# Attention scores from f16 halves: three products in place of one f32 product

## The chip, the cores and the metric

The kernel runs on one core of one Trainium2 chip. The core has five engines that each work through a queue of their own in order and meet through semaphores: TensorE (PE; its weight loads are shown apart as PEld), VectorE (DVE), ScalarE (ACT), GpSimd (POOL) and SyncE (SP, which only starts transfers). The metric is the device time of one launch in microseconds, lower is better.

## The reference

`x` is (4, 1024, 256) f32, the context (4, 64, 256). One layer, in two halves:

```
q = layernorm(x) @ w_qs[h]          # 16 heads of 64
k, v = ctx @ w_ks[h], ctx @ w_vs[h]
attn = softmax(q @ k.T)             # over the 64 context rows, no scaling
out = (attn @ v) * q                # times q, elementwise
x = x + tanh(g_xattn) * (concat(out) @ w_proj.T + b_proj)
logits = layernorm(x) @ gate_w.T    # 8 experts, the best 2 per token
y = sum over the 2 of softmax weight * (silu(x @ w1[e]) @ w2[e])
x = x + tanh(g_ffn) * y
```

The result is compared at f32 precision, so a product of two f32 matrices is either run in f32 or as three products of f16 halves (high by high, high by low, low by high).

## The kernel before, in words

**Two stages.** `attention` runs first and takes some 357 us, `experts` follows on the same core and takes the rest (71 blocks of 128 tokens). The change lies in `attention`, but for one call in `experts`.

**Tiling of attention.** The 4096 tokens are 8 groups of 512 (g = 0 to 7), two for each batch row. The 16 heads are 8 pairs (p = 0 to 7); a pair fills 128 partitions. So there are 64 steps, n = 8 g + p, and each engine has a function `step` that is run once for each n. The order inside a step is written out by hand and differs by engine; semaphores (waits like `pe.wait_ge(q_sb, n + 1)`) tie the engines together.

**What belongs to one step n**, by engine and in its order there:

- TensorE: q of pair n in six f16 products (L604); the scores of pair n-1 in f32 (`scores`, L614: four products 128x128x128, which the chip runs as eight); the transposes of the probabilities of n-4 (L625); probabilities times V of n-5 (L640); the output projection of n-6 in f16 halves (L656, L665); then a small job that depends on p (routing of group g-2, turning the next group's x).
- ScalarE: q from PSUM to f32 (`copy_q`, L816); copy of the transposed probabilities (L821); exponentials of n-2 (L826); at p 0, 1, 4 and 5 two LayerNorm tiles; the high half of a piece of an expert's weights (L867); the high half of the product of n-5 (`product_hi`, r_h, L832).
- VectorE: the sum of exponentials and its reciprocal, n-3 (L1021, L1024); LayerNorm and residual work by p; maximum and subtraction on the scores of n-1 (`score_max` L1010, `score_sub` L1015), with small routing jobs in the gaps between (`between`, gaps 1 to 4); attention times q, n-5 (`times_q`, r, L1030); the low half of the weight piece (L1067).
- GpSimd: probabilities normalized, n-3 (L1300); at p 3 and 7 an inverse deviation (L1278); one scatter of token records to memory (L1316), the first of a group behind the row numbers (`slots_done`); then the low half of the product of n-5 (`product_lo`, r_l, L1306), which waits for r_h.

Scores are single-buffered: `scores` waits until `score_sub` has read the pair before. The f32 K of all pairs, `kb`, is built in group 0 by `place_k` (ScalarE the lower, VectorE the upper 64 partitions).

**Routing of a group** runs two groups later: logits at p 2, best two experts at p 3, `both_masks` at p 4, and at p 5 `place_rows` (gap 1), `record_weights` (gap 2), `pick_rows` (gap 3, its first line updates `next_row`, which frees a PSUM bank that TensorE needs for turning x) and `row_numbers` (gap 4).

Of the kernel before, what the change touches and what calls it, by code (L numbers as in the profile page):

```python
# [30 lines left out]
P = 128  # L31
# [213 lines left out]
                            carry.next_row[:, :].unsqueeze(1).broadcast_to([P, TG, E]), ALU.add).then_inc(s.route_ops, 1)  # L245


def pick_rows(nc, dve, job_ps, r, s, carry, g):
    dve.wait_ge(s.route_ops, g * ROUTE + 5)
    nc.vector.tensor_tensor(carry.next_row[:, :], job_ps[:, TG * E:(TG + 1) * E], carry.next_row[:, :], ALU.add).then_inc(s.pos_read, 1)  # L250
    nc.vector.tensor_tensor(r.mask[:, :, :, :], r.pos[:, :, :].unsqueeze(1).broadcast_to([P, 2, TG, E]), r.mask[:, :, :, :],
                            ALU.mult).then_inc(s.route_ops, 1)

# [16 lines left out]
def attention(nc, ctx, dram, carry, weights):  # L270
# [8 lines left out]
    def sb(name, shape, dt):  # L279
        return ctx.enter_context(nc.sbuf_tensor(name, shape, dt))  # L280
# [4 lines left out]
    def sem(name):  # L285
        return ctx.enter_context(nc.semaphore(name))
# [1 line left out]

    wq_h, wq_l = (sb(f"wq_{s}", [P, KD, H * DK], F16) for s in "hl")
    wp_h, wp_l = (sb(f"wp_{s}", [P, NP, D], F16) for s in "hl")  # L290
    kb = sb("kb", [P, B, NP, 2 * M], F32)
    vb = sb("vb", [P, B, NP, 2, DK], F32)
    bias_rows = sb("bias_rows", [P, D], F16)
    bias_high = sb("bias_high", [64, D], F16)
# [15 lines left out]
    xn = carry.xn  # L310
    xt_h, xt_l = (sb(f"xt_{s}", [P, 2, KD, G], F16) for s in "hl")
    q32 = sb("q32", [P, NP, G], F32)
    smax = sb("smax", [P, 2, TG, 2], F32)
    ssub = sb("ssub", [P, 2, TG, 2, M], F32)
    ex = sb("ex", [P, 2, TG, 2 * M], F32)
# [51 lines left out]
        "base_set", "consts_set", "k_zeroed", "setup_ops", "tanh_done", "first_rows"))  # L367
    wp_hi, wp_lo, wq_hi, wq_lo, bias_hi = (sem(n) for n in ("wp_hi", "wp_lo", "wq_hi", "wq_lo", "bias_hi"))
    bias_zeroed, bias_lo = sem("bias_zeroed"), sem("bias_lo")
    k_mm, k_placed, v_mm, v_placed = (sem(n) for n in ("k_mm", "k_placed", "v_mm", "v_placed"))  # L370
    ln1_ops, ln1_rstd, ln1_shift, xn_done, xt_tp, xt_hi, xt_lo = (sem(n) for n in ("ln1_ops", "ln1_rstd", "ln1_shift", "xn_done", "xt_tp", "xt_hi", "xt_lo"))
    last_r_lo = sem("last_r_lo")
    q_mm, q_sb, s_mm, s_max, s_sub, e_x, pt_mm, e_sb = (sem(n) for n in (
# [166 lines left out]
    def _(pe):  # L540
# [22 lines left out]
        def project_k(p):  # L563

            pe.wait_ge(ctx_in, 16)
            pe.wait_ge(wk_in, 16)
            if p >= len(K_AT[0]):
                pe.wait_ge(k_placed, 2 * p)
# [37 lines left out]
            last.then_inc(q_mm, 1)  # L606

        def scores(b, n, p):
            pe.wait_ge(q_sb, n + 1)
            if isinstance(n, int) and n < NP:  # L610
                pe.wait_ge(k_placed, 2 * n + 2)
            after(pe, s_sub, n)
            for t in range(TG):
                last = nc.tensor.matmul(s_ps[:, t].rearrange("p h m -> p (h m)"), q32[:, p, t * P:(t + 1) * P],  # L614
                                        kb[:, b, p, :] if isinstance(b, int)
                                        else kb[:, bass.ds(b, 1), p, :].rearrange("p o m -> p (o m)"),
                                        start=True, stop=True)
# [68 lines left out]
        def small_job(g, k, p):  # L686

            if p == 1 and known(g, 2):
                x2_transpose(g - 2, k, 0)
            if p == 2 and known(g, 2):  # L690
                logits(g - 2)
            if p == 4 and known(g, 2):
                positions(g - 2)
            if p == 5 and has_next(g):
                if known(g, 2):
                    pe.wait_ge(routed.pos_read, g - 1)
                elif g == 0:
                    pe.wait_ge(k_placed, 2 * NP)
# [55 lines left out]
    def _(act):  # L754
# [35 lines left out]
        def place_k(p):  # L790

            act.wait_ge(k_mm, p + 1)
            if p == 0:
                act.wait_ge(k_zeroed, 2)
            nc.scalar.copy(k_place(kb, p, 0), k_batches(p, 0)).then_inc(k_placed, 1)

        def place_v(part):

# [10 lines left out]
        def copy_q(n, p):  # L809
# [5 lines left out]
            after(act, r_mul, n - NP + 1)  # L815
            nc.scalar.mul(q32[:, p, :], q_ps[:, :], 1.0 / WS).then_inc(q_sb, 1)  # L816

        def probs_out(n, p):
            act.wait_ge(pt_mm, n + 1)
            after(act, ot_mm, n - 1)  # L820
            nc.scalar.copy(e32[:, p % 2, :], pt_ps[:, :]).then_inc(e_sb, 1)  # L821

        def exps(n, p):
            act.wait_ge(s_sub, n + 1)
            after(act, p_nrm, n - 1)
            nc.scalar.activation(ex[:, p % 2].rearrange("p t m -> p (t m)"),  # L826
                                 ssub[:, p % 2].rearrange("p t h m -> p (t h m)"), ACT.Exp).then_inc(e_x, 1)
# [41 lines left out]
        def step(b, g, k, p, pairs_back=LAST):  # L869
# [64 lines left out]

    @block.vector
    def _(dve):
        nc.vector.memset(kb[:, 0:B // 2].rearrange("p b n m -> p (b n m)").bitcast(U32), 0).then_inc(k_zeroed, 1)
        nc.vector.memset(bias_rows[:, :].bitcast(U32), 0).then_inc(bias_zeroed, 1)

        def ln1(g, par):  # L940
# [54 lines left out]
        def place_k(p):  # L995

            dve.wait_ge(k_mm, p + 1)
            if p == 0:
                dve.wait_ge(k_zeroed, 2)
            nc.vector.tensor_copy(k_place(kb, p, 1), k_batches(p, 1)).then_inc(k_placed, 1)  # L1000

        def split_wp(part):

# [121 lines left out]
        def between(g, k, p, gap):  # L1125
# [14 lines left out]
            if p == 3:  # L1140
# [5 lines left out]
                    best_experts(nc, dve, route, routed, g - 2)  # L1146
                if gap == 4:
                    choice_masks(nc, dve, route, routed, carry, g - 2)
            if p == 4 and gap == 1:
                both_masks(nc, dve, route, routed, g - 2)  # L1150
            if p == 5:
                if gap == 1:
                    place_rows(nc, dve, job_ps, route, routed, carry, g - 2)
                if gap == 2:
                    record_weights(nc, dve, route, routed, carry, g - 2, rec[k])
                if gap == 3:
                    pick_rows(nc, dve, job_ps, route, routed, carry, g - 2)
# [75 lines left out]
        for p in range(LAST):  # L1233
            n = NS + p
            if p < 3:
                exp_sum(n - 3, NP + p - 3)
            if p < 1:
                score_max(n - 1, NP + p - 1)
                score_sub(n - 1, NP + p - 1)
            if p == 2:  # L1240
                dve.wait_ge(carry.rows_in[0], BLOCK_LOADS)
                turn_rows(nc, carry.xt, carry.rows, 0).then_inc(carry.x_turned, 1)
            if p < 5:
                times_q(n - 5, NP + p - 5)
# [14 lines left out]
    def _(pool):  # L1259
# [59 lines left out]
        def step(g, k, p, pairs_back=LAST):  # L1319
# [37 lines left out]
def experts(nc, ctx, dram, carry, loads_base, weights):  # L1357
# [240 lines left out]
    def _(dve):  # L1598
# [54 lines left out]
        def routing(j, i):  # L1653
# [24 lines left out]
            if i == 7:  # L1678
# [134 lines left out]
```

## Time and profile before

| what | value |
|---|---|
| median of three runs | 757.85 us (756.53 to 765.16) |
| the profiled execution | 760.15 us, its span 758.4 us |
| TensorE busy | 728.1 us (96% of the span) |
| VectorE busy | 586.2 us (77%) |
| ScalarE busy | 377.6 us (50%) |
| GpSimd busy | 397.4 us (52%) |
| mean granted TensorE clock | 0.995 |
| f32 score products L614 | 512, 67.5 us busy |

The busy times are sums over both stages, and a busy TensorE counts its products from start to end although they overlap. For the change only attention's stretch matters, and in it the place of each step: when its scores start, and when the last piece of GpSimd's work of that step ends.

### The profile page before, as it was taken

What the parts mean: (1) busy time and instruction counts of PE and PEld (TensorE: products, weight loads), DVE (VectorE), ACT (ScalarE), POOL (GpSimd) and SP (SyncE); (2) the same over time, 40 slices, a digit from 0 to 9 for tenths busy, and PEclk for the clock granted to TensorE, in tenths of its full rate; (3) what the DMA queues carried; (4) which work ended last, traced back from release to release, by engine and by line L of the source; (5) the groups of instructions that cost most, each with busy time, mean ns of one, the idle gap of its engine ahead of it and who ended that gap; (6) DMA issues with size and microseconds to landing.
All of it is one profiled execution on the core that took longest, in us unless ns stands there. A gap on an engine that the chain in (4) does not pass through costs nothing.

```text
span 758.4 us, 23508 instructions
## 1 busy us (share of the span) xinstructions
PE 728.1 (96%) x7980; PEld 605.2 (80%) x7981; DVE 586.2 (77%) x1270; ACT 377.6 (50%) x671; POOL 397.4 (52%) x308
## 2 busy tenths in 40 slices
PE   7999999999999999998899999999999999999994
PEld 6567767767677766776899988999999999999993
DVE  5688879798897989796778778776767677777761
ACT  3686776767677667754344432333333333333331
POOL 5145445767576666674533648444444353444434
PEclk9999999999999999999999999999999999999998
DMA  8552353536282625433888885333333333333322
GB/s 293 161 145 108 140 167 116 180 128 225 77 286 78 231 98 182 153 116 93 254 224 223 228 205 123 53 52 50 49 49 49 50 47 54 49 51 49 51 37 29
DMA packets 93177, 93.88 MB, mean 124 GB/s; under 512 B 59312, under 2 KB 77936, under 8 KB 92720
## 3 DMA queue, kind: packets, MB, share of 16 engines
q1 hardware_dynamic: 31184, 64.97, 25.8%
q0 software_dynamic: 13392, 18.03, 13.7%
q10 hardware_dynamic: 48528, 9.92, 7.6%
q8 instruction: 43, 0.70, 0.4%
q14 instruction: 30, 0.25, 0.1%
HBM read 53.89 MB, written 37.95 MB: 121 GB/s over the span
## 4 chain that ended last, share of the span: by engine, by line
DMA 40%; issue 7%; POOL 3%; PE 1%; ACTq 1%; DVE 1%; ACT 1%; POOLq 0%; DVEq 0%
DMA out<-y,meta 40%; POOL records L1757 2%; POOL out L1751 1%; PE h_ps L1484 0%; ACTq L158 0%; ACT y L1556 0%; ACT hid L1549 0%; PE h_ps L1528 0%; DVE last_stats L1659 0%; DVE ht_l L1629 0%; POOLq L70 0%; ACTq L160 0%; DVE ht_h L1627 0%; ACTq L1535 0%; DVE bx L165 0%
## 5 line engine op out<-in xcount | busy, mean ns | idle before, releaser
L1751 POOL DMA_INDIRECT out<-y,meta x71 | 157.4, 2217 | 198.4 <-DMA out<-y,meta 178.8
L1484 PE MATMUL h_ps<-bx_h,w_now 128*128 128x128 f16 x2272 | 194.7, 219 | 3.0 <-DVE bx_l L1615 1.6
L1497 PE MATMUL pair_ps<-weights,ht_h 128*128 x1136 | 190.7, 273 | 1.9 <-issue 1.3
L1484 PEld LDWEIGHTS h_ps<-bx_h,w_now 128*128 128x128 f16 x2272 | 152.6, 98 | 6.8 <-DVE bx_l L1615 2.6
L1484 PE MATMUL h_ps<-bx_l,w_now 128*128 128x128 f16 x1136 | 156.4, 219 | 0.9 <-issue 0.9
L1497 PE MATMUL pair_ps<-weights,ht_l 128*128 x568 | 154.8, 273 | 0.0
L1497 PEld LDWEIGHTS pair_ps<-weights,ht_h 128*128 128x128 f16 x1136 | 110.2, 97 | 17.9 <-issue 3.4
L1556 ACT ACTIVATE y<-pair_ps,meta 128x256 f32<-128x256 f32 x71 | 33.7, 475 | 172.3 <-DVE meta L1610 114.8
L1306 POOL TENSOR_TENSOR r_l<-r,r_h 128x512 f16<-128x512 f32 x62 | 75.3, 1215 | 73.6 <-ACT r_h L832 71.7
L1627 DVE CAST ht_h<-hid 128x1024 f16<-128x1024 f32 x71 | 50.1, 706 | 81.5 <-ACT hid L1549 76.6
L1549 ACT ACTIVATE hid<-h_ps 128x1024 f32<-128x1024 f32 x71 | 72.7, 1023 | 62.7 <-PE h_ps L1484 59.6
L1629 DVE TENSOR_TENSOR ht_l<-hid,ht_h 128x1024 f16<-128x1024 f32 x71 | 87.0, 1225 | 2.4
L1484 PEld LDWEIGHTS h_ps<-bx_l,w_now 128*128 128x128 f16 x1136 | 87.3, 98 | 0.8 <-issue 0.8
L1621 DVE COPY w_now<-weights 128x4096 f16 x71 | 87.3, 1229 | 0.2 <-DVE loads_base L1650 0.2
L1300 POOL TENSOR_TENSOR pn<-ex,rinv 128x512 f32<-128x512 f32 x64 | 66.5, 1039 | 30.9 <-DVE rinv L1024 30.9
L614 PEld LDWEIGHTS s_ps<-kb,q 128*128 128x128 f32 x512 | 67.1, 191 | 9.3 <-issue 0.7
L614 PE MATMUL s_ps<-kb,q 128*128 128x128 f32 x512 | 67.5, 275 | 0.3 <-DVE ssub L1015 0.3
L656 PE MATMUL pair_ps<-wp_h,r_h 128*128 128x256 f16 x256 | 61.3, 275 | 0.8 <-ACT r_h L832 0.8
L656 PE MATMUL pair_ps<-wp_l,r_h 128*128 128x256 f16 x256 | 60.7, 273 | 0.0
L1497 PEld LDWEIGHTS pair_ps<-weights,ht_l 128*128 128x128 f16 x568 | 55.6, 98 | 5.2
L1010 DVE TENSOR_REDUCE smax<-s_ps 128x8 f32<-128x512 f32 x64 | 43.2, 675 | 17.7 <-PE s_ps L614 17.0
L821 ACT COPY e<-pt_ps 128x512 f32<-128x512 f32 x64 | 37.4, 585 | 36.0 <-PE pt_ps L625 36.0
(250 smaller groups left out, 1235.9 us busy)
## 6 DMA issues: line engine op xcount, KB each, us to landing
stage<-in_w SPq DMA_DIRECT2D x16, 1024.0 KB
w_split<-split SPq DMA_DIRECT2D x14, 1024.0 KB, 6.5
weights<-w_split SPq DMA_DIRECT2D x14, 1024.0 KB
rows<-records ACTq DMA_DIRECT2D x268, 32.0 KB
xin<-in_x SPq DMA_DIRECT2D x7, 512.0 KB, 5.4
x_even<-in_x SPq DMA_DIRECT2D x4, 512.0 KB
x_odd<-in_x SPq DMA_DIRECT2D x4, 512.0 KB
out<-x_even SPq DMA_DIRECT2D x4, 512.0 KB
```

What stands on the lines that cost most here:

```text
L614: last = nc.tensor.matmul(s_ps[:, t].rearrange("p h m -> p (h m)"), q32[:, p, t * P:(t + 1) * P], kb[:, b, p, :] if isinstance(b, int) els ...
L656: nc.tensor.matmul(pj_ps[:, t, :], r_h[:, p % 2, t * P:(t + 1) * P], wt[:, p, :], start=(p == 0 and i == 0 and t % 2 == 0), stop=False, sk ...
L1010: nc.vector.tensor_reduce(smax[:, p % 2], s_ps[:, :, :, :], AX.X, ALU.max).then_inc(s_max, 1)
L1300: nc.gpsimd.tensor_tensor(pn[:, p % 2].rearrange("p h t m -> p t h m"), ex[:, p % 2].rearrange("p t (h m) -> p t h m", h=2), rinv[:, p % 2 ...
L1306: nc.gpsimd.tensor_tensor(r_l[:, p % 2, :], r32[:, p % 2, :], r_h[:, p % 2, :], ALU.subtract).then_inc(r_lo, 1)
L1484: last = nc.tensor.matmul(h_ps[r % 2][:, c, :], w1_now[:, r % 2, s, k * F + c * P:k * F + c * P + P], xt[:, r % 2, k, :], start=(j == 0 an ...
L1497: last = nc.tensor.matmul(y_ps[r % 2], ht[:, r % 2, c, :], weights_at(e, s, WN // 2 + c * D, D).rearrange("p o n -> p (o n)"), start=(c == ...
L1549: nc.scalar.activation(hid[:, r % 2], h_ps[r % 2][:, :, :], ACT.Silu, scale=1.0 / WS).then_inc(h_act, 1)
L1621: nc.vector.tensor_copy(w1_now[:, r % 2], weights[:, bass.ds(e, 1), :, 0:KD * F].rearrange("p o s n -> p (o s) n")).then_inc(w1_ready, 1)
L1627: nc.vector.tensor_copy(ht_h[:, r % 2], hid[:, r % 2]).then_inc(h_hi, 1)
L1629: nc.vector.tensor_tensor(ht_l[:, r % 2], hid[:, r % 2], ht_h[:, r % 2], ALU.subtract).then_inc(h_lo, 1)
L1751: pool.indirect_dma_start(out, bass.IndirectOffsetOnAxis(meta[:, r, 0:1].bitcast(U32), 0), y[:, r % 2, :], None, compute_op=ALU.add).then_ ...
```

## The change

Scores become three f16 products. `q_high` (ScalarE, behind `copy_q`) makes q_h = f16(q32); `q_low` (GpSimd, the last instruction of its step) makes q_l = f16(q32 - q_h). K is kept as two f16 arrays scaled by 64 (`WS`), and the exponential divides by 64. TensorE first runs eight products with q_h (for K's high and low half), then waits for q_l and runs four more with K's high half. The other part moves three small jobs on VectorE: `place_rows` from p 5, gap 1 to p 4, gap 4; the `next_row` update from `pick_rows` into `count_rows` at p 5, gap 1; and in the drain after the last group the rest of the block table goes to earlier steps, ahead of a wait for rows.

```diff
-def pick_rows(nc, dve, job_ps, r, s, carry, g):
+def count_rows(nc, dve, job_ps, s, carry, g):
+    dve.wait_ge(s.route_ops, g * ROUTE + 5)
+    nc.vector.tensor_tensor(carry.next_row[:, :], job_ps[:, TG * E:(TG + 1) * E], carry.next_row[:, :], ALU.add).then_inc(s.pos_read, 1)
+def pick_rows(nc, dve, r, s, g):
...
-    kb = sb("kb", [P, B, NP, 2 * M], F32)
+    kb_h, kb_l = (sb(f"kb_{s}", [P, B, NP, 2 * M], F16) for s in "hl")
+    q_h, q_l = (sb(f"q_{s}", [P, 2, G], F16) for s in "hl")
...
         def scores(b, n, p):
-            pe.wait_ge(q_sb, n + 1)
+            pe.wait_ge(q_hi, n + 1)
...
             for t in range(TG):
-                last = nc.tensor.matmul(s_ps[:, t]..., q32[:, p, t * P:(t + 1) * P], kb[:, b, p, :], start=True, stop=True)
+                for i, kb in enumerate((kb_h, kb_l)):
+                    nc.tensor.matmul(s_ps[:, t]..., q_h[:, p % 2, t * P:(t + 1) * P], kb[:, b, p, :],
+                                     start=(i == 0 and t == 0), stop=False, skip_group_check=True)
+            pe.wait_ge(q_lo, n + 1)
+            for t in range(TG):
+                last = nc.tensor.matmul(s_ps[:, t]..., q_l[:, p % 2, t * P:(t + 1) * P], kb_h[:, b, p, :],
+                                        start=False, stop=True, skip_group_check=True)
             last.then_inc(s_mm, 1)
...
+        def q_high(n, p):                        # ScalarE, in step n right behind copy_q
+            act.wait_ge(q_sb, n + 1)
+            after(act, s_mm, n - 1)
+            nc.scalar.copy(q_h[:, p % 2, :], q32[:, p, :]).then_inc(q_hi, 1)
...
         def place_k(p):                          # VectorE; ScalarE's: mul by WS into kb_h, then_inc(k_hi)
-            nc.vector.tensor_copy(k_place(kb, p, 1), k_batches(p, 1)).then_inc(k_placed, 1)
+            nc.vector.tensor_scalar(k_place(kb_h, p, 1), k_batches(p, 1), WS, None, ALU.mult).then_inc(k_upper, 1)
+            dve.wait_ge(k_hi, p + 1)
+            nc.vector.scalar_tensor_tensor(k_place(kb_l, p, 0), k_batches(p, 0), WS, k_place(kb_h, p, 0), ALU.mult, ALU.subtract)
+            dve.wait_ge(k_upper, p + 1)
+            nc.vector.scalar_tensor_tensor(k_place(kb_l, p, 1), ...).then_inc(k_lo, 1)
...
+        def q_low(n, p):                         # GpSimd
+            pool.wait_ge(q_hi, n + 1)
+            after(pool, s_mm, n - 1)
+            nc.gpsimd.tensor_tensor(q_l[:, p % 2, :], q32[:, p, :], q_h[:, p % 2, :], ALU.subtract).then_inc(q_lo, 1)
...
             if pairs_back >= 5:
                 product_lo(n - 5, (p - 5) % NP)
+            q_low(n, p)
...
-            if p == 4 and gap == 1:
-                both_masks(nc, dve, route, routed, g - 2)
+            if p == 4:
+                if gap == 1:
+                    both_masks(nc, dve, route, routed, g - 2)
+                if gap == 4:
+                    place_rows(nc, dve, job_ps, route, routed, carry, g - 2)
             if p == 5:
                 if gap == 1:
-                    place_rows(nc, dve, job_ps, route, routed, carry, g - 2)
+                    count_rows(nc, dve, job_ps, routed, carry, g - 2)
```

## Rows read from the trace of the kernel before

**Rows 1.** Busy time by stretch; engine columns, TensorE's granted clock, DMA share, GB/s.

```profile
8.00:10.00 2.00, 1.02 (x9) 0.82 (x7) 0.77 (x4) 0.43 (x1) 1.77 (x8) 1.00 1.02 416
...
259.70:301.20 41.50, 40.52 (x346) 29.11 (x345) 35.97 (x98) 29.37 (x54) 27.95 (x28) 1.00 0.46 154
```

**Rows 2.** Timeline, TensorE's scores, group 6 and the next start; start, length, us.

```profile
259.67 1.05 PE L614 MATMUL s_ps<-kb,q 128*128 128x128 f32 x8
264.31 1.05 PE L614 MATMUL s_ps<-kb,q 128*128 128x128 f32 x8
269.77 1.05 PE L614 MATMUL s_ps<-kb,q 128*128 128x128 f32 x8
275.50 1.05 PE L614 MATMUL s_ps<-kb,q 128*128 128x128 f32 x8
280.13 1.05 PE L614 MATMUL s_ps<-kb,q 128*128 128x128 f32 x8
284.88 1.05 PE L614 MATMUL s_ps<-kb,q 128*128 128x128 f32 x8
...
291.50 1.05 PE L614 MATMUL s_ps<-kb,q 128*128 128x128 f32 x8
...
296.61 1.05 PE L614 MATMUL s_ps<-kb,q 128*128 128x128 f32 x8
301.24 1.05 PE L614 MATMUL s_ps<-kb,q 128*128 128x128 f32 x8
```

**Rows 3.** Timeline, GpSimd's r_l of the same eight steps; last, idle before it.

```profile
264.41 1.15 POOL L1306 TENSOR_TENSOR r_l<-r,r_h 128x512 f16<-128x512 f32 x1 [0.42 <-ACT r_h L832]
...
269.30 1.15 POOL L1306 TENSOR_TENSOR r_l<-r,r_h 128x512 f16<-128x512 f32 x1 [1.58 <-ACT r_h L832]
...
274.01 1.15 POOL L1306 TENSOR_TENSOR r_l<-r,r_h 128x512 f16<-128x512 f32 x1 [1.40 <-ACT r_h L832]
...
279.69 1.58 POOL L1306 TENSOR_TENSOR r_l<-r,r_h 128x512 f16<-128x512 f32 x1 [1.27 <-ACT r_h L832]
...
286.20 1.15 POOL L1306 TENSOR_TENSOR r_l<-r,r_h 128x512 f16<-128x512 f32 x1 [1.81 <-ACT r_h L832]
...
291.95 1.17 POOL L1306 TENSOR_TENSOR r_l<-r,r_h 128x512 f16<-128x512 f32 x1
...
295.74 1.15 POOL L1306 TENSOR_TENSOR r_l<-r,r_h 128x512 f16<-128x512 f32 x1 [0.46 <-ACT r_h L832]
...
302.23 1.17 POOL L1306 TENSOR_TENSOR r_l<-r,r_h 128x512 f16<-128x512 f32 x1
```

**Rows 4.** Timeline, VectorE and ScalarE, the step whose scores start at 291.50.

```profile
293.00 0.68 DVE L1010 TENSOR_REDUCE smax<-s_ps 128x8 f32<-128x512 f32 x1
...
294.32 0.68 DVE L1030 TENSOR_TENSOR r<-ot_ps,q 128x512 f32<-128x512 f32 x1
...
295.03 0.62 ACT L832 CAST r_h<-r 128x512 f16<-128x512 f32 x1 [0.38 <-DVE r L1030]
```

**Rows 5.** Timeline, VectorE's maximum in the steps p 4, 5 and 7.

```profile
282.03 0.64 DVE L1010 TENSOR_REDUCE smax<-s_ps 128x8 f32<-128x512 f32 x1
...
287.08 0.64 DVE L1010 TENSOR_REDUCE smax<-s_ps 128x8 f32<-128x512 f32 x1
...
298.22 0.67 DVE L1010 TENSOR_REDUCE smax<-s_ps 128x8 f32<-128x512 f32 x1
```

**Rows 6.** Timeline, TensorE in the experts' stage, f16 products 128x128x128.

```profile
564.19 0.39 PE L1484 MATMUL h_ps<-bx_h,w_now 128*128 128x128 f16 x4
...
564.53 0.39 PE L1484 MATMUL h_ps<-bx_h,w_now 128*128 128x128 f16 x4
```

**Rows 7.** Groups by line, attention: the same subtraction on VectorE; busy, mean ns.

```profile
L1247 DVE TENSOR_TENSOR r_l<-r,r_h 128x512 f16<-128x512 f32 x2 | 1.4, 692 | 1.4 <-ACT r_h L832 1.4
```

**Rows 8.** Timeline, TensorE's scores: start of group 1 and of group 2.

```profile
54.95 1.05 PE L614 MATMUL s_ps<-kb,q 128*128 128x128 f32 x8
...
93.41 1.05 PE L614 MATMUL s_ps<-kb,q 128*128 128x128 f32 x8
```

More of the change, by code:

```diff
@@ L369, in attention @@
     bias_zeroed, bias_lo = sem("bias_zeroed"), sem("bias_lo")
-    k_mm, k_placed, v_mm, v_placed = (sem(n) for n in ("k_mm", "k_placed", "v_mm", "v_placed"))
+    k_mm, k_hi, k_upper, k_lo, v_mm, v_placed = (sem(n) for n in ("k_mm", "k_hi", "k_upper", "k_lo", "v_mm", "v_placed"))
+    q_hi, q_lo = sem("q_hi"), sem("q_lo")
     ln1_ops, ln1_rstd, ln1_shift, xn_done, xt_tp, xt_hi, xt_lo = (sem(n) for n in ("ln1_ops", "ln1_rstd", "ln1_shift", "xn_done", "xt_tp", "xt_hi", "xt_lo"))
@@ L567, in project_k @@
             if p >= len(K_AT[0]):
-                pe.wait_ge(k_placed, 2 * p)
+                pe.wait_ge(k_lo, p)
             for k in range(KD):
@@ L608, in scores @@
         def scores(b, n, p):
-            pe.wait_ge(q_sb, n + 1)
-            if isinstance(n, int) and n < NP:
-                pe.wait_ge(k_placed, 2 * n + 2)
+            pe.wait_ge(q_hi, n + 1)
+            if n < NP:
+                pe.wait_ge(k_lo, n + 1)
             after(pe, s_sub, n)
             for t in range(TG):
[L614 to L617, printed above, removed]
+                for i, kb in enumerate((kb_h, kb_l)):
+                    nc.tensor.matmul(s_ps[:, t].rearrange("p h m -> p (h m)"), q_h[:, p % 2, t * P:(t + 1) * P], kb[:, b, p, :],
+                                     start=(i == 0 and t == 0), stop=False, skip_group_check=True)
+            pe.wait_ge(q_lo, n + 1)
+            for t in range(TG):
+                last = nc.tensor.matmul(s_ps[:, t].rearrange("p h m -> p (h m)"), q_l[:, p % 2, t * P:(t + 1) * P], kb_h[:, b, p, :],
+                                        start=False, stop=True, skip_group_check=True)
             last.then_inc(s_mm, 1)
@@ L697, in small_job @@
                 elif g == 0:
-                    pe.wait_ge(k_placed, 2 * NP)
+                    pe.wait_ge(k_lo, NP)
                 x_transpose(g + 1, 0, job_ps)
@@ L793, in place_k @@
             if p == 0:
-                act.wait_ge(k_zeroed, 2)
-            nc.scalar.copy(k_place(kb, p, 0), k_batches(p, 0)).then_inc(k_placed, 1)
+                act.wait_ge(k_zeroed, 3)
+            nc.scalar.mul(k_place(kb_h, p, 0), k_batches(p, 0), WS).then_inc(k_hi, 1)
         def place_v(part):
@@ L826, in exps @@
             nc.scalar.activation(ex[:, p % 2].rearrange("p t m -> p (t m)"),
-                                 ssub[:, p % 2].rearrange("p t h m -> p (t h m)"), ACT.Exp).then_inc(e_x, 1)
+                                 ssub[:, p % 2].rearrange("p t h m -> p (t h m)"), ACT.Exp, scale=1.0 / WS).then_inc(e_x, 1)
         def product_hi(n, p):
@@ L879, in step @@
                     place_k(v)
+            q_high(n, p)
             if p == 2 and known(g, 2):
@@ L936, in _ @@
     def _(dve):
-        nc.vector.memset(kb[:, 0:B // 2].rearrange("p b n m -> p (b n m)").bitcast(U32), 0).then_inc(k_zeroed, 1)
+        nc.vector.memset(kb_h[:, :].rearrange("p b n m -> p (b n m)").bitcast(U32), 0).then_inc(k_zeroed, 1)
         nc.vector.memset(bias_rows[:, :].bitcast(U32), 0).then_inc(bias_zeroed, 1)
@@ L998, in place_k @@
             if p == 0:
-                dve.wait_ge(k_zeroed, 2)
-            nc.vector.tensor_copy(k_place(kb, p, 1), k_batches(p, 1)).then_inc(k_placed, 1)
+                dve.wait_ge(k_zeroed, 3)
+            nc.vector.tensor_scalar(k_place(kb_h, p, 1), k_batches(p, 1), WS, None, ALU.mult).then_inc(k_upper, 1)
+            dve.wait_ge(k_hi, p + 1)
+            nc.vector.scalar_tensor_tensor(k_place(kb_l, p, 0), k_batches(p, 0), WS, k_place(kb_h, p, 0), ALU.mult, ALU.subtract)
+            dve.wait_ge(k_upper, p + 1)
+            nc.vector.scalar_tensor_tensor(k_place(kb_l, p, 1), k_batches(p, 1), WS, k_place(kb_h, p, 1), ALU.mult, ALU.subtract).then_inc(k_lo, 1)
         def split_wp(part):
@@ L1156, in between @@
                 if gap == 3:
-                    pick_rows(nc, dve, job_ps, route, routed, carry, g - 2)
+                    pick_rows(nc, dve, route, routed, g - 2)
                 if gap == 4:
@@ L1239, in _ @@
                 score_sub(n - 1, NP + p - 1)
+            if p < 5:
+                times_q(n - 5, NP + p - 5)
+            if p in (1, 2, 3):
+                rest_of_table(p + 3)
             if p == 2:
@@ L1242, in _ @@
                 turn_rows(nc, carry.xt, carry.rows, 0).then_inc(carry.x_turned, 1)
-            if p < 5:
-                times_q(n - 5, NP + p - 5)
             if p in (3, 4):
@@ L1247, in _ @@
                 nc.vector.tensor_tensor(r_l[:, (p - 5) % 2, :], r32[:, (p - 5) % 2, :], r_h[:, (p - 5) % 2, :], ALU.subtract).then_inc(last_r_lo, 1)
-            if p == 3:
-                rest_of_table(4)
             if p == 4:
@@ L1252, in _ @@
                 nc.vector.tensor_tensor(carry.xt_l[:, 0], carry.xt[:, :, :], carry.xt_h[:, 0], ALU.subtract).then_inc(carry.x_lo, 1)
-                rest_of_table(5)
-        rest_of_table(6)
         carry.first_expert = dve.value_load(carry.table[0:1, 0:1], min_val=0, max_val=E - 1)
@@ L1272, in _ @@
         nc.gpsimd.memset(minus_half[:, :], -0.5).then_inc(consts_set, 1)
-        nc.gpsimd.memset(kb[:, B // 2:B].rearrange("p b n m -> p (b n m)").bitcast(U32), 0).then_inc(k_zeroed, 1)
+        for c in range(2):
+            nc.gpsimd.memset(kb_l[:, c * B // 2:(c + 1) * B // 2].rearrange("p b n m -> p (b n m)").bitcast(U32), 0).then_inc(k_zeroed, 1)
         def ln_rstd(i, g, ops, done):
@@ L1682, in routing @@
                 record_weights(nc, dve, route, routed, carry, j, rec[j])
-                pick_rows(nc, dve, job_ps, route, routed, carry, j)
+                count_rows(nc, dve, job_ps, routed, carry, j)
+                pick_rows(nc, dve, route, routed, j)
                 if j == 1:
```

## The prediction

> **What bounds the kernel now.** I read the busy times by stretch first. In group 6 TensorE is busy 40.52 of 41.50 us, VectorE 35.97, ScalarE 29.37, GpSimd 27.95 [rows 1]. The reader should see an attention stage in which TensorE runs without a break and the other three have slack, so their lateness costs nothing yet. Second, the timeline of TensorE's scores: eight steps from 259.67 to 301.24, 41.57 us, 4.6 to 6.6 us a step [rows 2]. Third, the timeline of the last long GpSimd instruction of the same steps, r_l [rows 3]. It ends well behind the next step's scores: r_l of the step that starts at 264.31 ends at 270.45, while the next scores started at 269.77. Nothing suffers from that, since its reader, the output projection, stands late in TensorE's step. The idle time before r_l is put down to r_h from ScalarE, and r_h in turn follows r on VectorE [rows 4]. So GpSimd has idle time, but it lies ahead of r_l, not behind it.
>
> **The new wait.** The change puts q_l of pair n behind r_l of pair n-5 in GpSimd's step n, and the first work of TensorE's step n+1 after q is the scores of pair n, whose last four products wait for that q_l. Follow it round: those products end, the maximum and subtraction of the same pair run on VectorE, and only then, in VectorE's order, r; then r_h on ScalarE, then r_l, then the next q_l on GpSimd, then the next scores. That is a ring with one turn per step. Before, scores needed q alone, and r_l fed nothing in it. From now on a step can't be shorter than one turn, however little TensorE has to do. Behind the waiting products on TensorE stand the transposes, probabilities times V (which r needs too) and the output projection; VectorE waits with its maximum in front of subtraction, r and weight piece.
>
> Is q_l late at once? In group 6's first step r_l ends at 265.56, and the next scores start at 264.31 [rows 2, 3]. With 1.15 us of q_l behind it, the low half would be there at 266.7, 2.4 us after the scores start; the eight high products cover about 0.5 of that. Late, then, in the first step, and the ring does the rest.
>
> **Pricing one turn.** The rows give most of a turn directly: from the start of a step's scores to the end of its r_l. With the start from [rows 2] and start plus duration from [rows 3], for p 0 to 7: 5.89, 6.14, 5.39, 5.77, 7.22, 8.24, 5.39, 6.79, sum 50.83 us. These hold every extra job of its step (LayerNorm tiles, routing, the first scatter that waits for the row numbers at p 5). Per step three things change:
> - The piece from scores start to scores end was 1.05 for f32 [rows 2]; only four f16 products lie in the ring, 0.39 [rows 6]. Minus 0.66.
> - q_l is added, the same shape and types as r_l: plus 1.15 [rows 3]. Below, VectorE does that subtraction in 0.69 [rows 7]; above, r_l once took 1.58 [rows 3]. I take 1.15, six of the eight rows within 0.02 of it.
> - The handover from GpSimd to TensorE is not shown; r_h ends at 295.65 and r_l starts at 295.74 [rows 3, 4], so 0.09.
>
> Together plus 0.58, times eight 4.64: 55.47. From that comes off what was mere backlog of VectorE, which would have time to clear while TensorE waits: the maximum started late against the end of its scores (start plus 1.05 plus 0.04) by 0.81 at p 4, 1.11 at p 5, 0.52 at p 7 [rows 2, 5] and 0.41 at p 6 [rows 2, 4]. Of the one at p 5 I take 0.6, because ScalarE's tiles hold the next part of that step up too. Sum 2.34. A group is then 53.1 us against 41.57: **plus 11.5**. A step without extras is p 6: 5.39 + 0.58 - 0.41 = 5.56.
>
> **The sum.** Groups 2 to 7 carry this order; I price the last like the others (it lacks the next group's LayerNorm but adds the block table): 6 x 11.5 = 69. Group 1 lasts 38.46 now [rows 8]; it has no scatter and no routing, so 8 x 5.56 = 44.5, plus two steps with LayerNorm tiles at 0.9 each (p 0 over p 6: 6.47 - 5.56), 46.3: plus 8. In group 0 three turns of the ring, some 1 us each, and building K as halves: 16 more VectorE instructions of at most a maximum's 0.68 [rows 4], a quarter of its size, so 0 to 11 us; 2.5, since most should fall into waits for loads and ScalarE. Plus 5.5. In all plus 82.5: 760.15 + 82.5 = 842.7 for an execution like the profiled one. That one lay 2.3 above the median of the runs shown, so **840 us**.
>
> **Edits at nothing.** q_h costs ScalarE about 0.62 a step, priced by r_h [rows 4], 5 us a group on 29.37 [rows 1] in a group of 53. It follows q, and q_l needs it only after r_l, some 4 us on; if that cover went, at most 0.62 x 62 = 38 us. TensorE's saving (below) falls into the wait. The moves of the row-number jobs free a bank sooner for turning x; TensorE has time there now, and `row_numbers` itself stays at gap 4 of p 5, so the first scatter, ahead of r_l and q_l on GpSimd, is no earlier. The table jobs moved in the drain: 0 to -1 us, taken as 0. Zeroing K writes the same bytes; WS rides on instructions that are there.
>
> Six products between the two starts of [rows 6] take 0.34, 57 ns each. The Trainium skill, TensorE: Matmul & The Clock Gate, Back-to-back issue gap, gives some 81 ns for such a product in a real stream with its weight loads; by it the four low products would take 0.1 us longer, 6 us in all. The trace does not bear that out.
>
> **Rivals.**
> 1. *q_l comes in time.* Then TensorE saves 1.05 less (0.39 + 8 x 0.057) = 0.2 us a step, 13 us, and the kernel takes 745. For it: TensorE has hardly a break [rows 1]. It decides where r_l's end plus 1.15 falls before the high products end, and there 2 us are missing. Chance 5%.
> 2. *Only GpSimd's load counts.* 27.95 + 8 x 1.15 = 37.2 fits into 41.5 [rows 1], so 757. Against it: the idle time lies ahead of r_l, and q_l is behind it. 3%.
> 3. *The ring turns, but the extra jobs slip out of it*: 8 x 5.56 = 44.5 a group, plus 2.9 in six groups, with groups 0 and 1 plus 29 in all: 787. For it: early inputs give ScalarE and VectorE more room. Against: LayerNorm tiles, routing and the first scatter stand in program order between scores and q_l. 6%.
> 4. *TensorE's clock falls*, because it now waits 1 to 3 us in each step. The granted clock is 1.00, the 2.4 GHz level, in group 6 without a break, but also where TensorE was busy 1.02 of 2.00 us [rows 1]. If it fell to 1.2 GHz throughout, TensorE's 40 us a group would be 80, 38 more in each of 8 groups: about 1060. The Trainium skill, the same page, A second HAM failure mode, has short waits between groups of products swing the clock between the two levels. The row with the half-busy engine speaks against it here. 3%.
>
> **How the numbers follow.** The ring with its extras: 83%, 840 us. Its own range: q_l at 0.69 takes 0.46 x 62 = 28 off, 812; at 1.58 it adds 27, 867; the whole backlog kept adds 14, inside that. 808 to 868 leaves out rivals 1 to 4, 17%, and so holds about 8 in 10. About 1% is what a measurement of this kernel can tell from no change: faster 5% (rival 1), same 3% (rival 2), slower 92%.
>
> **What would show it.** TensorE's wait before the low products named as GpSimd's q_l, 1 to 3 us in nearly every step of groups 1 to 7, longest at p 5; r_l directly followed by q_l; steps of 5.5 to 8 us, 53 a group; the experts' stage unchanged, about 400 us. I am wrong if q_l ends before the high products do, if scores start every 4.4 us, or if the long wait is named as q_h or K.

## The result: 842.5 us against 756.6, the ring as forecast

| what | before | after |
|---|---|---|
| median | 756.64 us (755.73 to 765.16) | 842.5 us (841.33 to 846.1) |
| ratio, with its 95% interval | | 1.1083 [1.1041, 1.1126] |
| profiled execution, span | 760.15, 758.4 us | 842.5, 840.8 us |
| TensorE, VectorE, ScalarE, GpSimd busy | 728.1, 586.2, 377.6, 397.4 us | 738.2, 598.7, 415.7, 461.6 us |
| mean granted clock | 0.995 | 0.978 |

The forecast was 840 us (842.7 for an execution like the profiled one). Lines of the kernel after: scores L622 (products with q_h) and L626 (with q_l), maximum L1031, subtraction L1036, r L1051, r_h L848, r_l L1335, q_h L832, q_l L1330.

**One turn of the ring**, timeline of the kernel after (start, length; in brackets the idle time before and who ended it), from the scatter of one p 5 to the scores after p 6:

```profile
302.66 0.19 POOL L1343 TENSOR_TENSOR wait_mark<-wait_mark 128x1 f32<-128x1 f32 x1 [3.56 <-DVE tok_ids L272]
303.00 1.00 POOL L1345 DMA_INDIRECT records<-rec_odd,slot_odd  x1
304.02 1.17 POOL L1335 TENSOR_TENSOR r_l<-r,r_h 128x512 f16<-128x512 f32 x1
305.13 1.16 POOL L1330 TENSOR_TENSOR q_l<-q,q_h 128x512 f16<-128x512 f32 x1
...
306.35 0.40 PE L626 MATMUL s_ps<-kb_h,q_l 128*128 128x128 f16 x4 [2.61 <-POOL q_l L1330]
306.79 0.69 DVE L1031 TENSOR_REDUCE smax<-s_ps 128x8 f32<-128x512 f32 x1 [1.63 <-PE s_ps L626]
307.51 0.69 DVE L1036 TENSOR_TENSOR ssub<-s_ps,smax 128x512 f32<-128x512 f32 x1
...
308.12 0.68 DVE L1051 TENSOR_TENSOR r<-ot_ps,q 128x512 f32<-128x512 f32 x1
308.83 0.62 ACT L848 CAST r_h<-r 128x512 f16<-128x512 f32 x1
309.54 1.15 POOL L1335 TENSOR_TENSOR r_l<-r,r_h 128x512 f16<-128x512 f32 x1 [1.09 <-ACT r_h L848]
...
310.66 1.15 POOL L1330 TENSOR_TENSOR q_l<-q,q_h 128x512 f16<-128x512 f32 x1
...
311.86 0.40 PE L626 MATMUL s_ps<-kb_h,q_l 128*128 128x128 f16 x4 [0.43 <-POOL q_l L1330]
```

Read down: each line starts within 0.15 us of the end of the line above it, except where the scatter waits for the row numbers. From 306.35 to 311.86 nothing but the ring sets the time: 5.51 us, with TensorE's f16 scores worth 0.40 of it. Against [rows 4] the order is the same; what is new is the last arrow, from q_l back to the scores.

**Who waits**, waits of the whole kernel after (us in total, times, longest):

```profile
POOL r_l L1335 <- ACT r_h L848: 93.1, 51, 4.7
PEld s_ps L626 <- POOL q_l L1330: 86.9, 57, 3.0
DVE smax L1031 <- PE s_ps L626: 79.9, 52, 3.1
PE s_ps L626 <- POOL q_l L1330: 77.1, 57, 2.8
```

The four are one chain seen from four engines, so they aren't added up. TensorE waits for q_l in 57 of 64 steps. VectorE's wait for scores is 79.9 us now; the list of the kernel before has

```profile
DVE smax L1010 <- PE s_ps L614: 17.0, 19, 1.6
```

so VectorE's backlog has gone.

**Where the time lies.** Timeline of the kernel after, the products with q_l at the ends of groups 0, 1, 5, 6 and 7:

```profile
63.00 0.40 PE L626 MATMUL s_ps<-kb_h,q_l 128*128 128x128 f16 x4 [1.43 <-POOL q_l L1330]
...
109.13 0.40 PE L626 MATMUL s_ps<-kb_h,q_l 128*128 128x128 f16 x4 [1.13 <-POOL q_l L1330]
...
318.65 0.51 PE L626 MATMUL s_ps<-kb_h,q_l 128*128 128x128 f16 x4 [2.19 <-POOL q_l L1330]
...
372.69 0.40 PE L626 MATMUL s_ps<-kb_h,q_l 128*128 128x128 f16 x4 [2.75 <-POOL q_l L1330]
...
423.02 0.40 PE L626 MATMUL s_ps<-kb_h,q_l 128*128 128x128 f16 x4 [2.21 <-POOL q_l L1330]
```

and of the kernel before, its last scores:

```profile
340.22 1.06 PE L614 MATMUL s_ps<-kb,q 128*128 128x128 f32 x8
```

Counted from end of scores to end of scores: group 0 ends at 63.40 against 56.00 [rows 8], plus 7.4; group 1 lasts 46.1 against 38.46, plus 7.7; groups 2 to 7 last 313.9 us (109.13 to 423.02) against 246.8 (93.41 to 340.22), plus 67.1. Together 82.2, and the spans differ by 82.4: the experts' stage is unchanged.

**Busy time by stretch**, kernel after: group 6, then stretches with a lower clock (columns as in [rows 1]):

```profile
318.70:372.70 54.00, 43.02 (x378) 28.07 (x379) 36.61 (x97) 34.17 (x62) 36.80 (x36) 0.94 0.35 118
44.00:46.00 2.00, 0.42 (x2) 0.42 (x3) 1.29 (x3) 2.00 (x5) 0.00 (x0) 0.93 0.99 255
46.00:48.00 2.00, 2.00 (x8) 1.05 (x7) 1.97 (x4) 1.59 (x4) 0.00 (x0) 0.50 0.87 342
48.00:50.00 2.00, 1.72 (x11) 0.78 (x9) 1.97 (x5) 1.37 (x4) 1.70 (x2) 0.71 0.31 29
252.00:260.00 8.00, 7.15 (x54) 4.89 (x54) 5.05 (x10) 3.68 (x7) 6.05 (x6) 0.79 0.91 316
```

No engine is full in group 6: 43.02 of 54 us on TensorE, 36.80 on GpSimd. That is what a ring looks like in such a table. The other four rows show a smaller effect: after a stretch in which TensorE was busy 0.42 of 2.00 us, the granted clock in the next row is 0.50, the 1.2 GHz level.

### The profile page after: what moved, and what is told of

The parts are those of the page before. It is cut to its first block and busy times, and to the rows that moved or that the text cites. A ratio compares the mean times of both kernels' runs of the same rounds, so it can differ in the third digit from the quotient of the medians.

```text
span 840.8 us, 24290 instructions
## 1 busy us (share of the span) xinstructions
PE 738.2 (88%) x8236; PEld 593.2 (71%) x8237; DVE 598.7 (71%) x1286; ACT 415.7 (49%) x735; POOL 461.6 (55%) x373
## 5 line engine op out<-in xcount | busy, mean ns | idle before, releaser
L1782 POOL DMA_INDIRECT out<-y,meta x71 | 151.2, 2130 | 206.7 <-DMA out<-y,meta 153.9
L1335 POOL TENSOR_TENSOR r_l<-r,r_h 128x512 f16<-128x512 f32 x62 | 74.9, 1208 | 93.4 <-ACT r_h L848 93.1
L1031 DVE TENSOR_REDUCE smax<-s_ps 128x8 f32<-128x512 f32 x64 | 44.2, 691 | 80.1 <-PE s_ps L626 79.9
L626 PE MATMUL s_ps<-kb_h,q_l 128*128 128x128 f16 x256 | 25.4, 222 | 77.1 <-POOL q_l L1330 77.1
L1330 POOL TENSOR_TENSOR q_l<-q,q_h 128x512 f16<-128x512 f32 x64 | 73.7, 1151 | 13.7 <-ACT q_h L832 13.7
L626 PEld LDWEIGHTS s_ps<-kb_h,q_l 128*128 128x128 f16 x256 | 14.8, 98 | 86.9 <-POOL q_l L1330 86.9
L666 PE MATMUL pair_ps<-wp_h,r_h 128*128 128x256 f16 x256 | 66.0, 289 | 0.0
L666 PE MATMUL pair_ps<-wp_l,r_h 128*128 128x256 f16 x256 | 65.5, 287 | 0.0
```

Source lines behind the costliest of these rows:

```text
L666: nc.tensor.matmul(pj_ps[:, t, :], r_h[:, p % 2, t * P:(t + 1) * P], wt[:, p, :], start=(p == 0 and i == 0 and t % 2 == 0), stop=False, sk ...
L1031: nc.vector.tensor_reduce(smax[:, p % 2], s_ps[:, :, :, :], AX.X, ALU.max).then_inc(s_max, 1)
L1330: nc.gpsimd.tensor_tensor(q_l[:, p % 2, :], q32[:, p, :], q_h[:, p % 2, :], ALU.subtract).then_inc(q_lo, 1)
L1335: nc.gpsimd.tensor_tensor(r_l[:, p % 2, :], r32[:, p % 2, :], r_h[:, p % 2, :], ALU.subtract).then_inc(r_lo, 1)
L1782: pool.indirect_dma_start(out, bass.IndirectOffsetOnAxis(meta[:, r, 0:1].bitcast(U32), 0), y[:, r % 2, :], None, compute_op=ALU.add).then_ ...
```

## The experiments

**1. Take q_l out of the ring.** q_low moves from the end of GpSimd's step to right behind the normalization, ahead of rstd, the scatter and r_l.

```diff
+            q_low(n, p)                 # right behind normalize
...
                 product_lo(n - 5, (p - 5) % NP)
-            q_low(n, p)
```

> The changed kernel with q_low moved up GpSimd's step, from behind r_l to right behind the normalizing, ahead of scatter and r_l. Same work on every engine. Theory (the ring scores - maximum - subtraction - r - r_h - r_l - q_l - scores sets the step): the ring is opened, TensorE waits for q_l a few tenths at most, and the steps go back to TensorE's length, 740 to 760 us. Rival (what costs is the added work: 1.15 us on GpSimd and 0.62 on ScalarE in every step, wherever they stand): above 820 us.

Measured: 772.78 us, 1.0182 [1.0143, 1.0222] of the kernel before. All but 14 of the 86 us come back by moving one line, so the place of q_l in its queue, far more than its work, made the change slow. TensorE's wait for q_l before these products, 77.1 us, is gone from the list (1.6 us are left before their weight loads). But the time lies 13 us above the expected range: in the trace groups 3 to 6 are 1.7 to 2.2 us longer than before, and the last 5.2. The timeline of one such group shows what is new (VectorE's two small jobs have 4 and 32 elements a partition):

```profile
147.31 1.17 POOL L1335 TENSOR_TENSOR r_l<-r,r_h 128x512 f16<-128x512 f32 x1
...
148.03 2.58 DVE L974 TENSOR_TENSOR vare<-vare,mv 128x4 f32<-128x4 f32 x1
...
148.43 1.05 POOL L1323 TENSOR_TENSOR pn<-ex,rinv 128x512 f32<-128x512 f32 x1
...
149.43 1.16 POOL L1330 TENSOR_TENSOR q_l<-q,q_h 128x512 f16<-128x512 f32 x1
...
158.10 1.17 POOL L1335 TENSOR_TENSOR r_l<-r,r_h 128x512 f16<-128x512 f32 x1
...
158.34 3.10 DVE L237 TENSOR_TENSOR mboth<-mask 128x32 f16<-128x32 f32 x1
...
159.22 1.05 POOL L1323 TENSOR_TENSOR pn<-ex,rinv 128x512 f32<-128x512 f32 x1
...
160.22 1.15 POOL L1330 TENSOR_TENSOR q_l<-q,q_h 128x512 f16<-128x512 f32 x1
...
161.49 0.19 PE L198 MATMUL job_ps<-mboth,before 128*128 128x32 f16 x1 [1.54 <-DVE mboth L237]
```

r_l, pn and q_l now follow each other without a gap. vare ends at 150.61 and q_l at 150.59; mboth ends at 161.44 and q_l at 161.37. Two jobs of some 0.2 us each (0.15 and 0.18 in the kernel after) hold VectorE until that run is over. They don't cost the same. The step p 2, in which vare is held, takes 5.68 us (146.55 to 152.23, scores to scores), 5.73 before [rows 2]. The step p 4, with mboth, takes 6.72 us (156.65 to 163.37) in place of 4.75, and TensorE's wait for mboth in it is 1.54. The eight steps around them, by stretch:

```profile
141.30:184.80 43.50, 39.76 (x381) 26.29 (x379) 41.02 (x98) 33.02 (x63) 37.28 (x35) 1.00 0.47 159
```

VectorE is busy 41.02 us of 43.50, against 35.97 of 41.50 in [rows 1].

**2. Make the disputed link longer.** Back in the kernel after, GpSimd does the subtraction twice, first into a spare tile.

```diff
+            nc.gpsimd.tensor_tensor(q_spare[:, :], q32[:, p, :], q_h[:, p % 2, :], ALU.subtract).then_inc(spare_done, 1)
             nc.gpsimd.tensor_tensor(q_l[:, p % 2, :], q32[:, p, :], q_h[:, p % 2, :], ALU.subtract).then_inc(q_lo, 1)
```

> The changed kernel with the subtraction of q_low run twice in a row by GpSimd, once into a spare tile. Theory: everything added between r_l and q_l's end lengthens every turn of the ring by its own length, 1.12 us in some 60 steps: 842 + 67 = about 910 us. Rival (GpSimd's queue has slack: about 37 us busy in a group of 52): 842 to 855 us.

Measured: 914.92 us, one run, 72.4 over the kernel after. In the traces groups 1 to 7 grow by 67.2 us, 1.20 for each of their 56 steps, where the added instruction takes 1.15; group 0 grows by 5.1. The whole link went into the time, and a little more; the mean granted clock is lower too (0.950 against 0.978). Its wait in the list of waits:

```profile
PE s_ps L627 <- POOL q_l L1333: 127.5, 55, 3.9
```

**3. The row numbers alone.** The f32 scores of before, with only the moved row and table jobs.

```diff
 (the kernel before)
+                if gap == 4:
+                    place_rows(nc, dve, job_ps, route, routed, carry, g - 2)   # at p 4
...
+                    count_rows(nc, dve, job_ps, routed, carry, g - 2)          # p 5, gap 1
```

> The kernel before with the moved row-number jobs and the moved table jobs alone, scores in f32 as before. Theory: TensorE's wait of 0.8 us for next_row at p 5, in five or six groups, goes: 4 to 5 us faster than before, 752 to 753 us. Rival (something else is as late there, or the earlier jobs delay the steps they move into): 756 to 760 us.

Measured: 755.22 us beside 758.97, 0.9957 [0.9932, 0.9982]. TensorE's wait for `next_row` is gone from the list; before it was

```profile
PE job_ps L547 <- DVE next_row L250: 4.0, 5, 0.8
```

So the part is worth some 3 us. That is above the 752 to 753 expected here and just under the rival's range; in the forecast it was worth nothing. The trace shows where some of it is lost: groups 2 to 6 are 0.65 to 0.82 us shorter than before, but the last is 1.2 us longer, and there one of the moved table jobs (past) takes 1.22 us in place of 0.20.

**4. The halves alone.** The kernel after with the row and table jobs back in their old places.

> The changed kernel with the row-number and table jobs back in their old places, scores from halves. Theory: TensorE waits for q_l anyway and p 5's turn is set by the row numbers at gap 4, so the same time, 840 to 845 us. Rival (the moved jobs shorten the ring at p 5): 847 us or more.

Measured: 845.93 us, 1.1131 [1.1089, 1.1172], beside 1.1083 [1.1041, 1.1126] for the whole change. That lies between the two expectations, and the intervals overlap: the halves carry the loss. The step p 5 takes the same in both traces (8.27 us here, 8.26 after, in group 2). The 3.4 us between the spans lie in whole groups: 2 and 3 take 54.7 and 54.6 us here, 52.0 after, and 4 takes 52.0 here, 53.5 after. In each of these the granted clock falls behind the wait at p 5 in the kernel with the longer group alone, so they can't be credited to the moves.

**5. Give TensorE more to do.** The eight products with q_h run twice.

```diff
+            for again in range(2):
+                for t in range(TG):
+                    ...                 # the eight products with q_h, the second time over the first
```

> The changed kernel with the eight high products run twice, the second set in place of the first: 0.45 us more work for TensorE in each step, ahead of the wait for q_l. Theory (the ring sets the step, the work falls into the wait): 840 to 847 us, the steps unchanged but those with the shortest waits, and where the clock fell behind the wait at p 5, fewer such falls, up to 6 us back. Rival (TensorE's own work still counts): 842 + 0.45 x 63 = 870 us.

Measured: 841.16 us, 1.108 [1.1013, 1.1148], no slower than after. TensorE's work fell into the wait, which its list shows shorter (77.1 in the kernel after). Groups 4 and 6, in which the clock falls behind p 5, still take 53.5 and 53.6 us:

```profile
PE s_ps L627 <- POOL q_l L1331: 56.8, 45, 2.4
```

**6. q_l between the scatter and r_l** (at p 5 ahead of the scatter), so that GpSimd's run has a scatter's gap in it.

> The changed kernel with q_low between the scatter and r_l (at p 5, where the scatter waits for the row numbers, ahead of the scatter). In e1, VectorE's small two-input jobs vare and mboth took 2.58 and 3.10 us, each ending as GpSimd's run of r_l, pn and q_l ended. Theory (a GpSimd run without a gap holds them; the scatter between pn and q_l opens one): mboth and vare fall to 1.2 us or less, a group to some 40 us, 745 to 757 us. Rival (VectorE is simply full, or the ring closes again through the later q_l): 768 to 800 us.

Measured: 811.23 us, 1.0678 [1.0634, 1.0721]: beyond both. mboth fell to 0.70 us, as meant, but the ring half closed again: TensorE waits 21.4 us in 17 times for q_l. Its longest steps are those at p 7, 9.47 us (184.48 to 193.95): there rstd stands ahead of q_l on GpSimd and waits 2.35 us for VectorE's vare, and TensorE waits 2.93 us for q_l. And VectorE's hold moved to other jobs with two inputs from SBUF, above all the low half of the weight piece, 0.69 us in the kernel before. How the 38 us over run 1 divide between the two isn't settled. Waits, then groups by line, of this kernel:

```profile
PE s_ps L626 <- POOL q_l L1330: 21.4, 17, 2.9
```

```profile
L1088 DVE SCALAR_TENSOR_TENSOR split<-stage,split 128x512 f16<-128x512 f32 x45 | 51.4, 1141 | 18.7 <-ACT split L883 18.7
```

**7. A short gap ahead of q_l.** Run 1, with q_l waiting for the end of pn.

> e1 with one more wait on GpSimd: q_low waits until the normalizing right ahead of it has ended, which was back to back with it. Same work, same order. Theory (VectorE's small two-input jobs wait for any gap in GpSimd's run): mboth falls from 3.1 to about 2 us and vare likewise, some 2 us a group, 758 to 766 us. Rival (the gap of a wait is too short, or the hold has another cause): mboth 3.1 us, 771 to 776 us.

Measured: 774.73 us, no better than run 1: the rival's number. vare falls to 1.47 us, but mboth only to 2.88, not to about 2. The gap did let both in:

```profile
148.78 1.47 DVE L974 TENSOR_TENSOR vare<-vare,mv 128x4 f32<-128x4 f32 x1
149.18 1.05 POOL L1323 TENSOR_TENSOR pn<-ex,rinv 128x512 f32<-128x512 f32 x1
150.31 1.16 POOL L1330 TENSOR_TENSOR q_l<-q,q_h 128x512 f16<-128x512 f32 x1
...
158.42 2.88 DVE L237 TENSOR_TENSOR mboth<-mask 128x32 f16<-128x32 f32 x1
...
160.20 1.05 POOL L1323 TENSOR_TENSOR pn<-ex,rinv 128x512 f32<-128x512 f32 x1
```

vare now ends at 150.25, with pn (150.23), before q_l begins at 150.31. mboth ends at 161.30, also with pn (161.25); it begins sooner than in run 1 against GpSimd's work, while the scatter ahead of r_l still runs, and is held through that as well. Eight steps take 43.7 us, as in run 1: p 4 falls to 5.97 us, p 5 rises to 7.10 (6.56 in run 1), and the shorter hold of vare at p 2 saves nothing (5.78).

**8. Other forms for the held jobs.** Run 1, with mboth as a `tensor_reduce` over the two masks (a sum; the text below says maximum) and vare as a `tensor_scalar` with one input.

```diff
-    nc.vector.tensor_tensor(r.mboth[:, :, :], r.mask[:, 0], r.mask[:, 1], ALU.add).then_inc(s.m_done, 1)
+        nc.vector.tensor_reduce(r.mboth[:, :, :], r.mask[:, :, :, :].rearrange("p c t e -> p t e c"), AX.X, ALU.add).then_inc(s.m_done, 1)
...
-            nc.vector.tensor_tensor(vare[:, 0, :], vare[:, 0, :], mv[:, 0, :, 1], ALU.add).then_inc(ln1_ops, 1)
+            nc.vector.tensor_scalar(vare[:, 0, :], mv[:, 0, :, 1], EPS, None, ALU.add).then_inc(ln1_ops, 1)
```

> The kernel with q_low ahead of the row numbers, and two small VectorE jobs written with one SBUF input each: mboth as a maximum over the two masks, vare as mv's variance plus a constant. Theory (a VectorE job with two SBUF inputs is held while GpSimd's r_l, pn and q_l follow each other without a gap): both jobs fall from 2.6 and 3.1 us to about 0.2, the group falls from 43.5 to 40 to 41.5 us, and the kernel takes 745 to 762 us. Rival (any VectorE job is held in that stretch, or the next two-input job in line takes the wait over): the group stays above 42.5 us and the kernel takes 765 to 775.

Measured: 771.26 us, 1.0176 [1.0127, 1.0225]; the rival's number. The timeline says which half of the theory fell:

```profile
148.02 2.59 DVE L975 TENSOR_SCALAR vare<-mv 128x4 f32<-128x4 f32 x1
...
158.09 1.17 POOL L1336 TENSOR_TENSOR r_l<-r,r_h 128x512 f16<-128x512 f32 x1
...
158.32 0.21 DVE L238 TENSOR_REDUCE mboth<-mask 128x32 f16<-128x64 f32 x1
...
159.04 2.34 DVE L979 SCALAR_TENSOR_TENSOR shift<-mv,rstd 128x4 f32<-128x4 f32 x1
```

mboth, 0.2 us after the same r_l began as in run 1, took 0.21 us in place of 3.10: this `tensor_reduce` isn't held. vare with one input still took 2.59: "two inputs" was too narrow. And shift, next in line with two inputs, took the wait over. The step p 4 falls to 5.01 us, but p 5 rises to 7.59 (6.56 in run 1): there TensorE waits 1.4 us for xn, which needs shift. The Trainium skill, SBUF — State Buffer, section Who interferes with whom, says which jobs can be held: on this chip `tensor_reduce` never meets GpSimd at their shared ports, while a `tensor_scalar` can, under conditions on its operands, and so can a job with two inputs from SBUF while GpSimd's instruction reads SBUF. These three durations agree.

**9. The same two forms on the f32 scores** (run 3 plus run 8's edit).

> The kernel with f32 scores and the row numbers a gap sooner, and the same two small VectorE jobs with one SBUF input each. Theory: mboth falls from 0.70 to about 0.2 us and vare by less; VectorE is not what the steps wait for except around the tables, so 0 to 2 us off: 0 to 0.3% faster than with the row numbers alone, 0.992 to 0.996 of the kernel before. Rival: the two jobs lie beside other work and nothing changes, 0.996 of it; above 1.0 would say that the one-input forms cost more than they save.

Measured: 752.21 us, 0.9929 [0.9895, 0.9962], the fastest kernel here and the one to keep. mboth takes 0.21 us in place of 0.70 in run 3. Beside run 3's 0.9957 [0.9932, 0.9982] the intervals overlap, so the times don't settle its share; in the traces groups 3 to 6 are 0.33 us shorter than run 3's (40.57 against 40.90).

**10. All three small jobs as `tensor_reduce`**: run 8, with vare a sum over two columns (variance, a constant) and shift a product over three (-1, rstd, mean).

```diff
+    ln = sb("ln", [P, 2, TG, 5], F32)          # -1, rstd, mean, variance, EPS
+            nc.vector.tensor_reduce(vare[:, 0, :], ln[:, 0, :, 3:5], AX.X, ALU.add).then_inc(ln1_ops, 1)
+            nc.vector.tensor_reduce(shift[:, 0, :], ln[:, 0, :, 0:3], AX.X, ALU.mult).then_inc(ln1_shift, 1)
```

> The kernel with q_low ahead of the row numbers, and all three small VectorE jobs of a group that were held there written as tensor_reduce (mboth a sum over the two masks, vare a sum over variance and a constant column, shift a product over a column of -1, rstd and mean). In the run before, the tensor_reduce form of mboth took 0.21 us where the two-input form took 3.1, while vare as a tensor_scalar with one input was still held 2.6 us and shift then 2.3. Theory (a tensor_scalar and a job with two inputs are held by GpSimd's gapless run, a tensor_reduce is not, and VectorE's time is what the step lacks): each of the three takes 0.1 to 0.3 us, VectorE is busy some 36 to 37 of the 44 us, the group takes 40 to 42 us, and the kernel 745 to 762 us. Rival (the next such job in line, the expert split or the record's weights, takes the wait over, or the steps are bound by something else): the three are short but the kernel stays at 765 to 772.

Measured: 763.17 us, 1.004 [1.0015, 1.0065], 10 us faster than run 1 and 1 us past the theory's upper edge. The three jobs take 0.15 to 0.21 us, and the steps p 4 and p 5 4.55 and 5.43 (in group 3). Eight steps of it, by stretch, and the scores that bound its last group:

```profile
186.40:228.00 41.60, 39.55 (x382) 26.42 (x380) 38.01 (x100) 33.23 (x63) 37.94 (x36) 1.00 0.48 165
```

```profile
300.48 0.39 PE L628 MATMUL s_ps<-kb_h,q_l 128*128 128x128 f16 x4
...
344.85 0.39 PE L628 MATMUL s_ps<-kb_h,q_l 128*128 128x128 f16 x4
```

The eight steps take 41.6 us, as before the change: freed of the ring and of these three holds, the f16 scores bring nothing. Beside run 9, with f32 scores and the same moved jobs, they even cost 1.0 us (40.57). TensorE, VectorE and GpSimd are all busy 37.9 us or more of the 41.6, VectorE more than the 36 to 37 expected; which of them sets the length isn't shown. At 300.48 this kernel is still 0.8 us ahead of before (301.24, [rows 2]); its last group then takes 44.4 us against 39.0. There the block table's jobs are longer in their turn:

```profile
317.83 2.02 DVE L1100 TENSOR_TENSOR count<-next_row,region_start 1x8 f32<-1x8 f32 x1
...
326.61 0.98 DVE L1111 TENSOR_TENSOR past<-block_no,full_ends 1x64 f32<-1x64 f32 x1
...
328.95 1.21 DVE L1116 TENSOR_TENSOR past<-past,full 1x64 f32<-1x64 f32 x1
```

Before, the three took 0.11, 0.20 and 0.20 us. The 3.7 us between are most of the last group's 5.4, if VectorE sets the time there, which isn't shown. 1.0 of them isn't of the halves: the last of the three takes 1.22 us in runs 3 and 9 too, with f32 scores. Giving them other forms was not tried.

## Why the prediction was right, step by step

- **The ring.** Right, and shown three ways: run 1 opens it and 70 us go, run 2 lengthens one link by 1.15 us and 1.20 arrive in each step of groups 1 to 7, run 5 adds work on TensorE and nothing arrives.
- **One turn.** Priced 5.56 us for a step without extras, measured 5.51. q_l priced 1.15 (seven of the eight rows lie within 0.02 of it, not six), measured 1.151 in the mean of 64. Handover to TensorE priced 0.09, measured 0.05 (311.81 to 311.86). The step that holds the first scatter, priced 8.24 + 0.58 - 0.6 = 8.22, takes 306.35 - 298.16 = 8.19.
- **A group.** Priced 53.1; groups 2 to 7 take 52.3 in the mean. Plus 67.1 against 69 forecast. The last group, priced like the others, adds 11.4. Group 1 plus 7.7 against 8. Step by step in group 5, the measured turns lie within 0.08 us of the priced ones but at p 1 (6.40 against 6.72) and p 4 (6.48 against 6.99).
- **Group 0 was mis-sized**: 7.4 against 5.5, and 4.1 of it is one step, p 5: 8.79 us (42.16 to 50.95), 4.64 before. In it TensorE's next job (45.58, L554) waits 2.00 us for kb_l, K's low half, and VectorE's maximum, behind kb_l in its order, starts 3.0 us after its scores end. So the term that was too small is K's halves. The clock falls there too: two q products together start every 0.86 us from 46.50 on and every 0.43 from 54.12 on, 1.3 us in three such pairs. That is the smaller part: in run 5 the granted clock is 1.00 in 44 to 52 us, with 0.45 us more work for TensorE, and the step still takes 8.34.
- **Rival 4 was half there.** The clock does fall behind some waits (0.50 in 46 to 48 us, 0.79 in 252 to 260), not throughout. Groups 4 and 6 take 53.50 and 54.04 us where 2, 3 and 5 take 52.0, 3.5 us together. In both the granted clock is 0.50 behind the wait at p 5 (254 to 257 and 360 to 363 us), and the step there takes 6.5 us in place of 5.5. A low clock doesn't always cost: it is 0.50 in 268 to 271 us too, and that step of group 5 takes 6.41, group 4's 6.40. I had put the effect at all or nothing; the sum had no term for it, and the slight excess of the ring's price covered it.
- **The size is in part luck.** 842.7 forecast for an execution like the profiled one and 842.5 measured lie closer than the terms: group 0 came out 1.9 us above its price and groups 2 to 7 1.9 below theirs, with 3.5 us in them that had no term.
- **An edit at nothing was not nothing.** The moved jobs bring 3 us on f32 scores (run 3). I saw that the bank comes free sooner and said TensorE has time there; before, it waited 4.0 us for `next_row`, a line of the list of waits that I did not use. q_h at nothing held: from 64 us on GpSimd's q_l waits for it nowhere in the list.
- **Rivals 1 and 2 were priced too low.** With q_l in time (run 1) the kernel takes 773, not 745, and not the 757 of GpSimd's plain load. That price added up each engine's busy time as if it were its own. With a denser GpSimd VectorE's jobs are longer, 41.02 us busy in eight steps against 35.97, and what TensorE pays is the held job that it waits for: mboth, 7.7 us in 5 times in run 1. Run 10, with the three holds gone, is 10 us faster.

Not settled: why the clock falls behind some waits of 2.6 us and not behind others of the same length (group 5's 2.61 us at 306.35 is followed by a step of 5.51, group 4's by one of 6.50).

## What to carry to other kernels

When work moves to an engine with idle time, ask where in its queue that idle time lies: behind an instruction that itself waits for the step's end, even 1.15 us closes a ring, and every link of the ring is then paid in full. Put such work ahead of the late instruction, and then look at which small jobs of VectorE have become long beside the dense engine, and which of them another engine waits for: here a job of 0.2 us was held for three instructions of GpSimd, and of two such jobs one cost time and the other none. As a `tensor_reduce`, none of the three rewritten jobs was held. And test the plain parts of a change alone: here the part thought to be worth nothing was the only one of the change to bring time.

## What the hardware showed that was not expected

- The same job, mboth, took 0.18 us in the kernel after, 0.70 before, 3.10 in run 1 and 0.21 as a `tensor_reduce` in run 8. A held job waits through several GpSimd instructions that follow without a gap (r_l, pn, q_l, 3.1 us). The 0.08 us that run 7 puts between pn and q_l let it in, in both places shown; the 0.04 us there between the scatter and r_l (159.05 to 159.09) did not, as far as GpSimd's rough spans can tell.
- The twelve f16 products of a step were as cheap as forecast: 0.055 us from one to the next with q_h, 0.40 for the four with q_l (0.39 in [rows 6]).
